# Two-layer graph attention on one core: largest weights shared through TensorE, unit 0 prepared by its own code, layer 1's weights loaded one by one, the last eight outputs on two banks

## The reference, cut to what matters

```python
h = jnp.maximum(_layernorm(x, axis=-1), 0.0)
q = _heads(h @ Wq + bq); k = _heads(h @ Wk + bk); v = _heads(h @ Wv + bv)   # 6 heads of 64
scores = jnp.einsum('bhqd,bhkd->bhqk', q, k) / np.sqrt(64)
probs = jax.nn.softmax(scores + jnp.where(adj, 0.0, -9e15)[:, None], axis=-1)
ctx = jnp.einsum('bhqk,bhkd->bhqd', probs, v)      # merged back to 384 features
x = x + ctx @ Wf + bf
```

## Time and profile before

| | |
|---|---|
| runs | 2121.31, 2118.20, 2116.44 us; median 2118.2 us |
| profiled execution, own time | 2120.55 us |
| its span, first to last instruction | 2118.6 us |
| PE (TensorE matmuls) busy | 2023.7 us, 96% |
| DVE, ACT, POOL busy | 1753.7, 1266.0, 1338.2 us |
| mean granted TensorE clock | 0.984 of full speed |

### The profile page before, as it was taken

One profiled execution on the slowest core, in us unless ns is written; L12 is line 12 of the kernel. 1 busy time (PEld: TensorE's weight loads), 2 busy tenths in 40 slices (PEclk: granted clock), 3 DMA queues, 4 the chain that ended last, 5 costly groups with the idle time before them and its releaser, 6 DMA issues.

```text
span 2118.6 us, 62046 instructions
## 1 busy us (share of the span) xinstructions
PE 2023.7 (96%) x18832; PEld 1220.1 (58%) x18832; DVE 1753.7 (83%) x6074; ACT 1266.0 (60%) x2249; POOL 1338.2 (63%) x1810
## 2 busy tenths in 40 slices
PE   1689999999999999999999999999999999999996
PEld 0356666666566566656665666666566665666653
DVE  4488888888888888888888888888888888888875
ACT  2266666666666566666666666666666666666652
POOL 3366666666666666666666666666666666666652
PEclk7899999999999999999999999999999999999998
DMA  5433444444444444444544444444444444444433
GB/s 155 124 85 105 111 116 135 134 133 117 127 132 135 130 131 121 129 129 131 137 134 124 115 132 129 136 131 136 115 131 131 136 134 135 130 115 117 115 94 94
DMA packets 443713, 264.91 MB, mean 125 GB/s; under 512 B 341987, under 2 KB 443365, under 8 KB 443365
## 3 DMA queue, kind: packets, MB, share of 16 engines
q1 hardware_dynamic: 443364, 260.76, 44.5%
HBM read 134.75 MB, written 125.83 MB: 123 GB/s over the span
## 4 chain that ended last, share of the span: by engine, by line
PE 45%; issue 24%; POOL 21%; DMA 4%; DVE 3%; SPq 2%; ACT 1%; POOLq 1%; DVEq 0%; ACTq 0%
PE ps_proj L467 8%; PE ps_proj L469 8%; PE ps_proj L468 8%; POOL x_tile L402 5%; POOL ht_lo L418 5%; PE ps_pt L510 5%; POOL ct_lo L406 5%; PE ps_out L467 4%; PE ps_out L468 4%; PE ps_out L469 4%; PE ps_scores L541 4%; POOL rstd L391 3%; DMA c_moved<-c_dram 3%; POOL probs L411 2%; POOL shift L393 1%
## 5 line engine op out<-in xcount | busy, mean ns | idle before, releaser
L411 POOL TENSOR_TENSOR probs<-probs,row_max 128x768 f32<-128x768 f32 x256 | 376.0, 1469 | 586.7 <-DVE row_max L822 586.7
L643 ACT ACTIVATE probs<-probs,exp_scale 128x768 f32<-128x768 f32 x256 | 239.7, 936 | 257.9 <-POOL probs L411 257.9
L800 DVE SCALAR_TENSOR_TENSOR qk_lo<-ps_proj,qk_bias,qk_hi 128x512 f16<-128x512 f32 x384 | 282.8, 737 | 130.8 <-ACT qk_hi L630 130.8
L822 DVE CUSTOM_DVE_ANT_0 probs<-ps_scores,mask 128x128 f32<-128x128 f32 x1536 | 342.4, 285 | 0.7 <-PE ps_scores L541 0.5
L599 ACT ACTIVATE pt_hi<-ps_pt 128x384 f16<-128x384 f32 x512 | 223.0, 487 | 151.1 <-PE ps_pt L510 150.9
L467 PE MATMUL ps_proj<-wv_hi,ht_hi 128*128 128x384 f16 x768 | 252.8, 329 | 43.4 <-DVE wv_lo L739 24.6
L630 ACT ACTIVATE qk_hi<-ps_proj,qk_bias 128x512 f16<-128x512 f32 x384 | 258.7, 674 | 31.5 <-PE ps_proj L469 31.4
L467 PE MATMUL ps_out<-wf_hi,ct_hi 128*128 128x384 f16 x768 | 251.8, 328 | 19.6 <-DVE ctx_n L812 12.4
L785 DVE TENSOR_TENSOR pt_lo<-ps_pt,pt_hi 128x384 f16<-128x384 f32 x512 | 260.3, 550 | 0.2 <-ACT pt_hi L599 0.2
L406 POOL TENSOR_TENSOR ct_lo<-c_moved,ct_hi 128x384 f16<-128x384 f32 x256 | 233.9, 914 | 37.3 <-ACT ct_hi L638 37.0
L402 POOL TENSOR_TENSOR x_tile<-x_tile,out_bias 128x384 f32<-128x384 f32 x256 | 255.9, 1000 | 1.9 <-DVE out_bias L745 1.9
(11 more groups left out here) (91 smaller groups left out, 5000.6 us busy)
## 6 DMA issues: line engine op xcount, KB each, us to landing
h_dram<-h_blocks SPq DMA_DIRECT2D x256, 192.0 KB, 1.9
h_moved<-h_dram SPq DMA_DIRECT2D x1024, 48.0 KB, 1.9
c_dram<-c_blocks SPq DMA_DIRECT2D x256, 192.0 KB, 1.9
c_moved<-c_dram SPq DMA_DIRECT2D x1024, 48.0 KB, 2.0
x_tile<-in_x SPq DMA_DIRECT2D x32, 768.0 KB, 5.3
out_x<-x_tile SPq DMA_DIRECT2D x128, 192.0 KB, 1.9
adj_u<-in_adj SPq DMA_DIRECT2D x64, 64.0 KB, 2.1
wq_raw<-in_L_gnn_Wq SPq DMA_DIRECT2D x2, 576.0 KB, 6.4
```

What stands on the lines that cost most here:

```text
L411: nc.gpsimd.tensor_tensor(probs[i % 2][:, :, :], probs[i % 2][:, :, :], row_max[i % 2][:, :].rearrange("p (a o) -> p a o", o=1) .to_broadc ...
L800: nc.vector.scalar_tensor_tensor(out=qk_lo[b][:, chunk, :], in0=ps_proj[bank_of("qk", chunk)][:, :], scalar=qk_bias[layer_of(t)][:, chunk ...
L822: ins = nc.vector.tensor_tensor_reduce(probs[i % 2][:, s, :], ps_scores[s // PAIRS][:, (s % PAIRS) * P:(s % PAIRS + 1) * P], mask[b][:, i, ...
```

## The change

1. **The maximum over partitions.** POOL's `setup` is gone. TensorE transposes `largest` [128, 6] into ps_out (`turn_largest`), DVE takes the maximum along each of the six rows (`peak`) and multiplies it into a 6 by 6 diagonal (`peaks`), TensorE multiplies a matrix of ones by it (`share_largest`), so that each partition of ps_out holds the six maxima, and DVE copies them to `largest_all`. TensorE's old `setup` is now `sum_out_bias`.
2. **The first unit** no longer goes through slots -3 and -2 (`FIRST` is -1). Each engine has straight code for unit 0 and the first graphs of unit 1. DVE takes the largest values between the second and the third block transpose, POOL takes the four norms ahead of the four h_lo, ACT interleaves h_hi with the high halves of the weights. The projections wait for the one weight they use rather than for all four.
3. **The loads.** Wv comes first. x of unit 1 is issued behind the first two graphs' hand-off, x of unit 2 behind the other two's. The other x tiles are loaded one at a time, in step 3 of the slot four units ahead, by the rule that tiles 7 and up had before. Layer 1's Wf, Wv, Wq and Wk are issued one by one between hand-offs of unit 1. Layer 1's output bias is summed in step (0, 0) and its scales are found in step (0, 1).
4. **The last two units** write their outputs to ps_proj0 and ps_proj1 in turn. `apply_probs` then waits for `ctx_ready` alone, and `output` for the residual sum two outputs back.

```diff
-    FIRST, LAST = -3, LAYERS * GROUPS
+    FIRST, LAST = -1, LAYERS * GROUPS
...
+        def out_bank(t, i):
+
+            return ps_out if t < LAST - 2 else ps_proj[i % 2]
...
# SP, slot
                     if (t, i) == (-1, 0):
-                        load_out_bias(1)
-                    if i == 3 and exists(t + 4) and layer_of(t + 4) == 0 and group_of(t + 4) >= X_BUFFERS:
+                        load_weight(1, 0)
+                    if (t, i) == (-1, 1):
+                        load_weight(1, 1)
+                    if i == 3 and exists(t + 4) and layer_of(t + 4) == 0:
                         load_x(t + 4, m)
...
# POOL
-            def setup(l):
-                pool.wait_ge(largest_found, 5 * (l + 1))
-                nc.gpsimd.partition_all_reduce(largest_all[:, :], largest[:, :], P,
-                                               bass.bass_isa.ReduceOp.max).then_inc(largest_shared, 1)
...
+            for i in range(PER):
+                norm(0, i, None)
+            for i in range(PER):
+                h_lo(0, i, None)
+            for i in range(2):
+                norm(1, i, None)
# PE
+            def turn_largest(l):
+                pe.wait_ge(largest_found, 5 * (l + 1))
+
+                wait(pe, scales_set, l)
+                pe.transpose(ps_out[0:6, 0:P], largest[:, :], ident[:, :]).then_inc(largest_turned, 1)
+
+            def share_largest(l):
+                pe.wait_ge(peaks_set, l + 1)
+                pe.matmul(ps_out[:, 0:6], ones[0:6, :], peaks[:, :], start=True, stop=True).then_inc(largest_shared, 1)
...
-                    if unit_no(t) <= AHEAD:
-                        pe.wait_ge(weights_set, 4 * (l + 1))
+                if c == 0 and chunk % KT == 0 and unit_no(t) <= AHEAD:
+                    pe.wait_ge(weights_set, 4 * l + CAST_ORDER.index(chunk // KT) + 1)
...
-                if exists(ou):
+                if exists(ou) and ou < LAST - 2:
                     pe.wait_ge(out_added, unit_count(ou, m, PER, oi + 1))
                 else:
                     wait(pe, ctx_ready, unit_count(t, m, PER, i))
+                if (t, i) == (0, 0):
+                    pe.wait_ge(scales_set, LAYERS)
...
-                cu, ci = graph_at(t, i, 2)
-                if exists(cu):
+                if t < LAST - 2:
+
+                    cu, ci = graph_at(t, i, 2)
                     pe.wait_ge(ctx_ready, unit_count(cu, m, PER, ci + 1))
                 else:
-                    pe.wait_ge(out_added, unit_count(t, m, PER, i))
+
+                    wait(pe, out_added, unit_count(t, m, PER, i - 1))
# ACT, ahead of slot -1
+            for i in range(PER):
+                relu(0, i, None)
+            for i in range(2):
+                h_hi(0, i, None)
+            weights_hi(0, CAST_ORDER[0])
+            weights_hi(0, CAST_ORDER[1])
+            h_hi(0, 2, None)
+            weights_hi(0, CAST_ORDER[2])
+            h_hi(0, 3, None)
+            weights_hi(0, CAST_ORDER[3])
# DVE
+            def find_peaks(l):
+                dve.wait_ge(largest_turned, l + 1)
+                then(nc.vector.tensor_reduce(peak[:, :], ps_out[0:6, 0:P], AX_X, ALU.max))
+                nc.vector.tensor_scalar(peaks[:, :], ident[0:6, 0:6], peak[:, :], None, ALU.mult).then_inc(peaks_set, 1)
```

More of the change, by code:

```diff
@@ L130, in over_slots @@
     def over_slots(eng, slot):
-        for t in range(FIRST + 2, LOOP_AT):
+        for t in range(FIRST, LOOP_AT):
             slot(t, None)
@@ L361, in _ @@
             load_x(0, None)
+            load_biases(0)
+            for j in CAST_ORDER:
+                load_weight(0, j)
             load_out_bias(0)
-            load_weights(0)
+            for i in range(2):
+                keep_blocks(0, i, h_blocked, h_blocks, h_dram, h_kept, h_back, None)
+            for i in range(2):
+                bring_back(0, i, h_dram, h_moved, h_kept, h_back, ht_set, None)
             load_x(1, None)
[L365 to L369, removed]
+            for i in range(2, PER):
+                keep_blocks(0, i, h_blocked, h_blocks, h_dram, h_kept, h_back, None)
+            load_adj(0, None)
+            for i in range(2, PER):
+                bring_back(0, i, h_dram, h_moved, h_kept, h_back, ht_set, None)
+            load_x(2, None)
+            load_biases(1)
+            load_out_bias(1)
+            keep_blocks(1, 0, h_blocked, h_blocks, h_dram, h_kept, h_back, None)
+            load_weight(1, 3)
+            bring_back(1, 0, h_dram, h_moved, h_kept, h_back, ht_set, None)
+            load_weight(1, 2)
             over_slots(sp, slot)
@@ L450, in _ @@
                                     base=0, pattern=[[-1, P]], channel_multiplier=1).then_inc(ident_set, 1)
-            slot(FIRST, None)
-            slot(FIRST + 1, None)
+            for i in range(PER):
+                norm(0, i, None)
+            for i in range(PER):
+                h_lo(0, i, None)
+            for i in range(2):
+                norm(1, i, None)
             over_slots(pool, slot)
@@ L679, in slot @@
                             qk_hi_out(t + 1, chunk, m)
-            slot(FIRST, None)
-            slot(FIRST + 1, None)
-            for j in CAST_ORDER:
-                weights_hi(0, j)
+            for i in range(PER):
+                relu(0, i, None)
+            for i in range(2):
+                h_hi(0, i, None)
[5 more added lines that the diff above has]
+            weights_hi(0, CAST_ORDER[3])
+            for i in range(2):
+                relu(1, i, None)
             over_slots(act, slot)
@@ L841, in slot @@
                     su, si = graph_at(t, i, 11)
-                    if (t, i) == (FIRST + 1, 2):
-                        spread_biases(0)
-                        for j in range(4):
-                            find_largest(0, j)
-                        find_scales(0)
                     if exists(hu):
@@ L870, in slot @@
                             qk_lo_out(t + 1, chunk, m)
-                    if (t, i) == (0, 2):
-                        find_scales(1)
-                    if (t, i) == (-1, 3):
-                        keep_out_bias(1)
             dve.wait_ge(consts_set, CONSTS)
-            slot(FIRST, None)
-            slot(FIRST + 1, None)
+            for i in range(PER):
+                statistics(0, i, None)
+                if i >= 2:
+                    h_turn(0, i - 2, None)
+            find_largest_bias(0)
+            for j in CAST_ORDER:
+                find_largest(0, j)
+            spread_v_bias(0)
+            find_peaks(0)
+            find_scales(0)
+            h_turn(0, 2, None)
+            h_turn(0, 3, None)
             for j in CAST_ORDER:
@@ L881, in _ @@
             keep_out_bias(0)
+            for i in range(3):
+                statistics(1, i, None)
+            h_turn(1, 0, None)
             over_slots(dve, slot)
```

64 lines of the change are left out of this document (42 added, 22 removed).

## The result

The changed kernel takes 2080.8 us (median of 4, 2078.88 to 2084.19) against 2118.3: a ratio of 0.9823, 95% interval 0.9806 to 0.9841. A second measurement on another chip gave 2081.9 against 2114.9, 0.9842 [0.9828, 0.9856]. The forecast was 2075.0 with a range of 2066 to 2088.

What follows compares the result with a forecast made beforehand. TensorE was busy 96%, its body full, so only start and end could move: 2118.6 - 36.8 (start) - 7.5 (end) = 2074.3 us of span, a median of 2073.9, plus 1 for gaps: 2075, range 2066 to 2088.

Steps and rivals of the forecast that it cites:

- the 1 that was added for gaps: Whole sum: 1 us added to the median of 2073.9 for semaphore gaps of the hand-worked chain.
- Part 1: Layer 0's scales: set at 19.7 us, 14 us earlier, with 1.9 for the hop between TensorE and DVE.
- Rival C: Layer 0's scales: TensorE's hop is no faster than POOL's, 7 us more, 2082; chance 0.04.
- Part 2: First q: starts at 29.1 in place of 51.24, 22.1 us earlier, bounded by the hand-off of h.
- Part 3: Slot -1: carries the earlier q through with nothing added, first score at 59.7 in place of 81.51, 21.8 us.
- Rivals A and D: Slot -1 paced by SP, 2085, chance 0.18; six loads each hold a hand-off like the bulk, 2142, chance 0.02.
- Part 4: Slot 0: gains 13.0 (POOL's second reduction), 3.0 (half clock) and 1.5 (layer 1's scales), loses 2.5 (bias sum).
- I take 1.5 as gained: Slot 0: layer 1's scales, one step earlier, give 1.5 of the 3.42 us wait.
- Part 5: The end: 7.5 us from slots 63 and 64 and the last hand-off, bounds 3 and 10.
- 1.6: Slot 64: the last context no longer waits for graph 0's residual sum, saving one output and one sum, 1.6 us.
- 1.4: Last hand-off: its return comes after about 2.2 us in place of 3.58, without a store ahead on SP, 1.4 us.
- rival B: The end is paced by the context's round trip and gains only 1 or 2 us, 2081; chance 0.09.

Runs made afterwards that it cites:

- e8: The changed kernel with POOL's low halves of unit 0 held until layer 0's scales are set; 2081.20 us, ratio 0.9835.
- e2: The changed kernel with POOL's reduction over partitions back in place of TensorE's sharing, loads' order and second bank kept; 2096.5 us, ratio 0.9913.
- e3: The kernel before with only the sharing of largest values moved from POOL to TensorE and DVE (layer 1's scales one step earlier); 2093.83 us, ratio 0.9892.
- e4: The changed kernel with x of units 3 to 6 and layer 1's four weights loaded in bulk ahead of slot -1; 2091.22 us, ratio 0.9885.
- e6: The changed kernel with DVE's layer 1 powers, scales and weight halves spread over slots 1, 2 and 3; 2076.76 us, ratio 0.9812.
- e1: The changed kernel with the last eight outputs back on one bank, contexts waiting again for residual sums; 2083.53 us, ratio 0.9849.
- a9: The changed kernel measured once more, unchanged, on another chip; 2081.94 us, ratio 0.9842 to the kernel before.
- e9: The changed kernel with 18, 12 and 15 unread filler matmuls ahead of the last three outputs' waits for ct_lo; 2078.37 us.

## Why the prediction was right or wrong

The direction and the range held, and so did the mechanism at the start; the end was mis-sized. The centre was 5.8 too fast: 3.95 at the start (36.8 forecast, 32.85 found), 3.4 at the end (7.5 forecast, 4.1 found between the profiles), less the 1 that was added for gaps and 0.5 between the gain of the medians and that of the spans.

**Part 1** held within 1 us. The reductions end at 15.35 (forecast 15.7), the hop takes 1.95 with the spread (15.35 to 17.3; taken 1.9, bounds 1.1 and 8.45). Scales set at 20.7 (19.7): the error is their own length, 3.38 for 2.08, which e8 lays on POOL. It cost nothing. **Rival C** falls: the hop takes less than POOL's first still stretch alone. (Its text puts 1.3 for the hop where part 1 has 1.9; the price would be 6.6 us, not 7.)

**Part 2**: return at 13.89 (14.1), fourth ht_hi at 28.34 (27.5), q at 30.34 (29.1); 20.9 gained for 22.1. The argument that POOL's wait of 26.6 us was the deeper cause of this part was too simple. e2 shows that with the new order POOL's first pair hardly counts (2.7), and e3 that with the old order it counts 9.4. The order of work and the sharing cover each other: each alone brings the start 20.1 (e2) or 22.2 us (e3) forward, both together 32.9.

**Part 3**: the first score came at 61.49 for 59.7, 1.8 late; 1.2 of it is q's, and slot -1 itself took 31.15 us from q to the first score for the 30.6 of the prediction. But this rests on the new order of the loads, to which the sum gave no number and which carried 8.6 (e4). **Rivals A and D** fall: one hand-off of slot -1 did take long beside the weights (store at 39.88, return at 45.41, 5.5 us where the others took about 2.0), but ht_hi waits at most 3.72 there, and the slot is 0.6 longer than forecast, not 10. The long wait of the earlier trace rows was the bulk's; e4 brings it back (13.76 at ht_hi, 11.04 at TensorE).

**Part 4**: 12.8 gained in slot 0 for 15.0. The wait of 13.04 and the half clock went as forecast (clock 1.00 from 56 to 97 us). The failed term is "I take 1.5 as gained" for the scales of layer 1. They take 3.97 us of DVE (73.59 to 77.56) in place of 2.1, with POOL beside them, and 2.56 of the 3.42 us stayed. With them moved away (e6) slot 0 takes 28.66, which is the 28.7 that the sum had; that it is so exact is luck, since the bias sum took 3.04 (62.10 to 65.14) for the 2.5 of the sum.

**Part 5** was mis-sized: "the step is DVE's 4.2: 1.1 saved in each of four steps" holds for three of the four steps of slot 63 (1.20, 1.25 and 1.20 saved against e1) and fails in the third. SyncE issues the context's hand-offs 4.8 to 5.6 us apart (2043.79, 2048.58, 2053.41, 2059.01), and in the third step TensorE waits 2.13 for the context: 5.75 us at the full clock (a9) and 7.02 here, in place of 5.32. The terms "1.6" and "1.4" for slot 64 failed whole: 3.0 forecast, 0.4 found (19.76 for 20.18), and against e1's 19.07 nothing. The last return did follow its hand-off earlier, 2.67 us (2067.81 to 2070.48) for the 3.58 of the earlier trace rows, but the time was lost elsewhere in the slot; DVE's waits there are for outputs that wait for ct_lo. What the second bank gave, 2.4 by the profiles with and without it, is close to the 1 or 2 of **rival B**, which had 0.09, and under the lower bound of 3. The 4.1 between the two profiles looks better than that by luck: before's profile has a step of 7.14 at a low clock.

The half clock at the end was in no case, though it is not new: the last output of before falls to 0.50 too (2114 to 2118), behind a wait of 3.94, and e1's last output takes 2.42 us in place of e9's 1.74. That the second bank makes it worse is not shown: the clock of the last outputs differs between the profiles with two banks (e2 has it at 1.00 until the last output).

Of the tests set, the scales "near 20" (20.7), q at 29 (30.34), the first score at 60 (61.49), no wait of TensorE over 5 us after 45 (the longest is 4.04) and a body busy over 99% were met. "Steps of 4.2" came near in three of four (4.55, 4.08, 4.13) and not in one (7.02). Two failed: the first score of unit 1 came at 92.39 for 88, and POOL does wait over 4 us after the scales, 6.45 at 27.00 and 4.54 at 42.04, for hand-offs that had not come.

## What to carry to other kernels

Where an engine stands still around an exotic instruction, look for the same result from engines that are idle at that time: five small operations of 0.16 to 0.59 us replaced 13 us of still stand, twice. Two edits to one start are not two terms of a sum: ask for each what it is worth when the other is done. When a step is made shorter, look for the next cycle that has its own period (here SyncE's store, wait, return), and look at the granted clock behind TensorE's last waits. One profile each is not enough for a few microseconds at the end: six profiles with the same code there spread over 2.5 us.

## What the runs showed of the hardware

- Some of DVE's short operations on small tiles in SBUF are held until a POOL operation beside them ends: 0.90 in place of 0.17 for a tensor_scalar of 128x4, gone when POOL is quiet (e8); in slot 0 two operations that write bound (128x3 and 128x2) took 0.53 and 0.77 in place of 0.17 and 0.15, and ended at 74.31 and 75.19 where POOL's ended at 74.29 and 75.17. Operations of 128x1 were not held (0.14 and 0.15). The Trainium skill, GPSIMD Engine Reference, section 8 (Key points), says that POOL shares its SBUF interfaces with VectorE, with contention for DVE's two-port modes or two inputs in SBUF; the trace agrees for the operation of 128x2, which reads two tiles; for the others it does not tell their mode. It gives the size, up to one POOL operation (0.9) for each.
- POOL's reduction costs 5.7 to 6.3 us ahead of it and 6.9 to 7.6 behind it each time it comes back among ordinary operations, four times in two kernels.
- A queue with bulk loads in it delays twice: 14 us to issue them and 7.4 in place of 2.0 for the small transfer behind them (e4; 14.4 and 7.1 in the kernel before).
- Throwaway matmuls in TensorE's waits kept the granted clock at 1.00 where it had been 0.50, and brought 2.1 us by the traces, 1.4 of it in the last output (e9).
